# Another order for the gated update's candidate, root and gate steps, and a row of ones set inside the second loop

## The chip, the cores and the metric

One core of a Trainium2 chip runs the whole kernel in one launch. The metric is the time of the launch in device microseconds (us); the number that counts is the median of a few runs. Below, PE is TensorE, DVE is VectorE, ACT is ScalarE, POOL is GpSimd and SP is SyncE.

## The reference

Four graph layers on 3,125 nodes of 64 channels and 100,000 edges, with a layer norm of the residual behind each one: attention over edges (L0), an aggregation with a gated update (L1), a two-step convolution with small dense layers (L2), a relational layer (L3). The change sits at the end of L1, whose part that matters is:

```python
h = jnp.concatenate([xi, xj, ea], axis=-1) @ Wpre + bpre      # per edge
agg = jnp.concatenate([mean, mn, mx, std], axis=-1)           # over each node's edges
out = jnp.concatenate([m, o1, o2, o3], axis=-1) @ Wpost + bpost
gi = out @ Wih + bih
gh = x @ Whh + bhh
r = sigmoid(ir + hr); z = sigmoid(iz + hz)
n = tanh(i_n + r * h_n)                                       # the candidate
x = layernorm(x + (1.0 - z) * n + z * x)                      # its root: sqrt(var + eps)
```

## The kernel before

Nodes lie in 25 blocks of 128, one node per partition. An edge step handles up to 16 edges of each node of one block. The first loop runs over the steps for L0, the second one for L1; each turn does two steps (u = 0 and 1), 31 turns here. The second loop has two parts. Its first 25 turns also count edge types and unpack a matrix of counts, one block a turn, which ScalarE stores to DRAM (`at_tab`). The other 6 turns do not. In a step VectorE adds the gathered rows (L1983), signals GpSimd that the buffer is free, multiplies by the edge weight (L1987), adds TensorE's edge terms (L1995) and reduces the step before it (L1972, L1976). ScalarE makes maxima and minima (L1255). GpSimd gathers rows with indirect DMAs (L558), SyncE loads indices and attributes.

After the loop comes the chunk stage. The 25 blocks form three chunks of 8, 8 and 9 blocks. For each chunk:

- `sums_of` (DVE): mean, variance, minimum, maximum; ScalarE takes a root (`chunk_std`, L1274).
- `transpose_sums` and `mix_sums` (PE), with ScalarE's copies between them (`copy_sums`, L1096).
- `out_of` (DVE, L2049 to L2052): takes the products into `sR`.
- `transpose_out` (PE), `copy_out` (ACT, L1096) into the tile `T1`, then `gate_products` (PE, L696), two blocks to a product group. `T1` has 64 rows of data and a 65th row, `T1[C:C+1]`, that must be one for the bias.
- `take_gates` (ACT, L1294 and L1295): sigmoid and copy of each product group; this also frees the bank.
- `state_of` (DVE): the candidate's two steps (L2059, L2061), then `ask`, which signals ScalarE for the tanh (`chunk_tanh`, L1300) and waits for its answer; four steps of the update (L2063 to L2069); `layernorm` (L1893 to L1905), which asks ScalarE for the root (`std`, L1203) in its middle.
- `split` (DVE, L2075 to L2083): the new values in three bf16 parts for the convolution. Chunk 1's split lets TensorE begin the convolution (L916), chunk 2's lets it go on. At the end of the last `state_of` a signal (`x_done`) releases SyncE's next loads of `at_tab` (L523) and GpSimd's gathers of edge counts.

Each engine runs its instructions in the order in which they are written; an instruction that waits holds all behind it. ScalarE and VectorE meet by two counters (`act_q` up at each request, `act_r` at each answer), so requests must be answered in the order in which they are made. The order of the chunk stage is written out by hand on each engine. TensorE's order is: sums 0, mix 0, sums 1, mix 1, out 0, gates 0, sums 2, mix 2, out 1, gates 1, out 2, gates 2. ScalarE's function tables are reloaded when sigmoid or tanh follow the root, or the root them (ACT_TABLE_LOAD).

The memory of `T1` serves as workspace while counts are unpacked and stored, so its row of ones can be set only when the last store has landed (`at_stored`). Before the change VectorE sets it between `sums_of(2)` and `out_of(0)` (L2090, L2091), and then copies two small tables (`reset_loop`, L1803, L1804).

Of the kernel before, what the change touches and what calls it, by code (L numbers as in the profile page):

```python
# [32 lines left out]
N, E, C, R = 3125, 100000, 64, 9  # L33
NB = 25
# [25 lines left out]
def build(nc, a, out):  # L60
# [18 lines left out]
    with ExitStack() as ctx:  # L79
# [6 lines left out]
        def at(off, parts, *shape, dt=F32):  # L86
            n = 1
            for s in shape:
                n *= s
            v = arena[0:parts, off:off + n]  # L90
            if dt != F32:
                v = v.bitcast(dt)
            if len(shape) == 2:
                v = v.rearrange("p (a b) -> p a b", b=shape[1])
            if len(shape) == 3:
                v = v.rearrange("p (a b c) -> p a b c", b=shape[1], c=shape[2])
            return v
# [49 lines left out]
        gates = [at(14100 + 9 * 4 * C * c, P, 9, 4 * C) for c in range(3)]  # L147
# [14 lines left out]
        T1 = sb("T1", [P, NP])  # L162
# [147 lines left out]
        pack_in, pack_split, pack_cast, at_stored = (  # L310
            sem(n) for n in ("pack_in", "pack_split", "pack_cast", "at_stored"))
# [776 lines left out]
        def _(act):  # L1088
# [3 lines left out]
            def copy_transposed(dst, n, width):  # L1092

                k = ring["tp"]
                act.wait_ge(tp_full, k + 1)
                act.activation(dst, tp[0:width, k % 2, 0:n], ACT.Copy).then_inc(tp_evac, 1)  # L1096
                ring["tp"] = k + 1
# [5 lines left out]
            def asked():  # L1103
                act.wait_ge(act_q, ring["q"] + 1)
                ring["q"] += 1

            n = 0
# [40 lines left out]
            k = 1 + len(PAIRS)  # L1148
# [51 lines left out]
            def std(lo=0, hi=NB):  # L1200

                asked()
                act.activation(S(STD_)[:, lo:hi], S(VAR_)[:, lo:hi], ACT.Sqrt, bias=epsb[:], scale=1.0 / C).then_inc(  # L1203
                    act_r, 1)
# [71 lines left out]
            def copy_sums(c):  # L1276
                lo = CHUNKS[c][0][0]
                for h in range(2):
                    for g in CHUNKS[c]:
                        copy_transposed(aggT[h][:, (g[0] - lo) * P:(g[-1] + 1 - lo) * P], P * len(g), P)  # L1280
# [5 lines left out]
            def take_gates(c, first, last):  # L1286
                lo = CHUNKS[c][0][0]
                for k in range(first, last):
                    pair = CHUNK_PAIRS[c][k]
                    bank = MM_GRU[c] + k  # L1290
                    b = slice(pair[0] - lo, pair[-1] + 1 - lo)
                    v = mm[:, bank % 2].rearrange("p (b c) -> p b c", c=4 * C)[:, 0:len(pair)]
                    act.wait_ge(mm_full, bank + 1)
                    act.activation(gates[c][:, b, 0:2 * C], v[:, :, 0:2 * C], ACT.Sigmoid)  # L1294
                    act.activation(gates[c][:, b, 2 * C:], v[:, :, 2 * C:], ACT.Copy).then_inc(mm_evac, 1)  # L1295

            def chunk_tanh(c):
                s = slice(CHUNKS[c][0][0], CHUNKS[c][-1][-1] + 1)
                asked()
                act.activation(sR[:, s], sR[:, s], ACT.Tanh).then_inc(act_r, 1)  # L1300
# [6 lines left out]
            copy_out(0)  # L1307
            act.wait_ge(sums_done, AGG + 2)
            take_gates(0, 0, 4)
            copy_sums(2)  # L1310
            copy_out(1)
            take_gates(1, 0, 4)
            chunk_tanh(0)
            copy_out(2)
            take_gates(2, 0, 3)
            std(0, 8)
            take_gates(2, 3, 5)
            chunk_tanh(1)
            std(8, 16)
            chunk_tanh(2)  # L1320
            std(16, 25)

# [53 lines left out]
            for s in range(NB):  # L1376
# [3 lines left out]
                for gi, g in enumerate(GROUPS):  # L1380
                    n = len(g)
# [33 lines left out]
        def _(dve):  # L1415
# [11 lines left out]
            def ask(ins):  # L1427

                ins.then_inc(act_q, 1)
                ring["q"] += 1  # L1430
                dve.wait_ge(act_r, ring["q"])
# [120 lines left out]
            for pair in PAIRS:  # L1552
                s = ring["stage"] % NSTAGE
                if ring["stage"] >= NSTAGE:
                    dve.wait_ge(stage_out[s], 16 * (ring["stage"] // NSTAGE))
                n = len(pair)
                k = ring["mm"]
# [360 lines left out]
            for half, done in zip(HALVES, (X1A, X1)):  # L1918
                lo, hi = half[0][0], half[-1][-1] + 1
                w = slice(lo, hi)  # L1920
                for g in half:
                    n = len(g)
# [56 lines left out]
            def step1(i, u, with_hist):  # L1979
                blk = block_in(word[u])  # L1980
                h = hh[u][:, :, 0:C]
                wait_rows(LOOP1, u)
                tt(h, G1[u], aR[:, bass.ds(blk, 1), :].to_broadcast([P, SLOTS, C]), ALU.add).then_inc(index_used, 1)  # L1983
                dve.wait_ge(attrs_in[u], 16 * (i + 1))
                prepare_step(2 * i + u + 1, 1 - u)
                d().then_inc(LOOP1.free, 1)
                tt(h, h, bc(ewm[u], C), ALU.mult)  # L1987
                tt(rel_hot[:], bc(relation[u], R), bm(relF[:], SLOTS), ALU.is_equal)
                d()
                red_(rel_sum[:], rel_hot[:].rearrange("p s r -> p r s"), X_AXIS, ALU.add)  # L1990
                d()
                v_ = accT[:, bass.ds(blk, 1), :]
                tt(v_, v_, rel_sum[:].unsqueeze(1), ALU.add)
                dve.wait_ge(edge_terms, 2 * i + u + 1)
                tt(h, h, mm[:].rearrange("p a (s c) -> p (a s) c", c=C), ALU.add).then_inc(h_ready, 1)  # L1995
                if with_hist:
                    type_hots(1, 2 * i + u + 2 * HI, 8 * (2 * i + u) + 16 * HI, u)
                if with_hist and u == 0:
                    dve.wait_ge(pack_in, 16 * (i + 1))
                    dve.wait_ge(pack_cast, i + 1)  # L2000
                    ts(even_sb, pack_sb, 0x070707, None, op0=ALU.bitwise_and)
                    ts(odd_sb, pack_sb, 3, 0x071F1F, op0=ALU.logical_shift_right, op1=ALU.bitwise_and)
                    ts(top_sb, pack_sb[:, 0:P], 22, 3, op0=ALU.logical_shift_right, op1=ALU.bitwise_and)
                    d().then_inc(pack_split, 1)
                add_step(2 * i + u, 1 - u)
                end_step(u)

            with aligned(dve, 0, HI) as i:
                for u in range(2):
                    step1(i, u, True)  # L2010
            with dve.Fori(HI, pairs) as i:
                for u in range(2):
                    step1(i, u, False)
# [8 lines left out]
            def range_of(c):  # L2022
                lo, hi = CHUNKS[c][0][0], CHUNKS[c][-1][-1] + 1
                return slice(lo, hi), hi - lo
# [17 lines left out]
            def out_of(c):  # L2042
                s, n = range_of(c)
                for k, g in enumerate(CHUNKS[c]):
                    bank = MM_AGG[c] + k
                    dve.wait_ge(mm_full, bank + 1)
                    w = slice(g[0], g[-1] + 1)
                    v = mm[:, bank % 2].rearrange("p (b c) -> p b c", c=2 * C)[:, 0:len(g)]
                    tt(mpR[:, w], mpR[:, w], v[:, :, 0:C], ALU.add)  # L2049
                    tt(sR[:, w], v[:, :, C:2 * C], bc(S(RATIO_)[:, w], C), ALU.mult).then_inc(mm_evac, 1)  # L2050
                d()
                tt(sR[:, s], sR[:, s], mpR[:, s], ALU.add)  # L2052
                d().then_inc(sums_done, 1)

            def state_of(c):
                s, n = range_of(c)
                gate = lambda k: gates[c][:, 0:n, k * C:(k + 1) * C]
                dve.wait_ge(mm_evac, MM_GRU[c] + len(CHUNK_PAIRS[c]))
                tt(sR[:, s], gate(0), gate(3), ALU.mult)  # L2059
                d()  # L2060
                tt(sR[:, s], sR[:, s], gate(2), ALU.add)  # L2061
                ask(d())
                tt(gate(0), x1R[:, s], sR[:, s], ALU.subtract)  # L2063
                d()
                tt(gate(0), gate(0), gate(1), ALU.mult)
                d()
                tt(gate(0), gate(0), sR[:, s], ALU.add)
                d()
                tt(sR[:, s], gate(0), x1R[:, s], ALU.add)  # L2069
                d()  # L2070
                layernorm(xN, sR, s.start, s.stop, scrC)
# [15 lines left out]
            ts(totI[:, 2:3], l3[:, 2, 0:1], float(E), None, op0=ALU.is_lt)  # L2087
            for c in range(3):
                sums_of(c)
            dve.wait_ge(at_stored, 16 * (NB + 1))  # L2090
            dve.memset(T1[C:C + 1], 1.0)  # L2091
            reset_loop()
            for c in range(3):
                out_of(c)
            ring["mm"] = MM_MLP[0]
            for c in range(3):
                state_of(c)
                if c == 2:
                    d().then_inc(x_done, 1)
                s, n = range_of(c)  # L2100
                split(parts2[:, s], xN[:, s], scrC[:, 0:n])
# [169 lines left out]
```

## Time and profile before

| | |
|---|---|
| median of 3 runs | 3,403.16 us (3,392.29 to 3,418.53) |
| the profiled execution's own time | 3,406.42 us |
| its span, first to last instruction | 3,404.6 us |
| busy: DVE, POOL, PE, ACT | 2,097.6, 1,803.9, 1,468.5, 1,244.7 us |
| mean granted clock of TensorE | 0.615 of full speed |
| border of the second loop's two parts | near 2,697 us |
| chunk stage | about 2,934 to 3,049 us |

The profile shows one execution. Its times count from the first instruction. A busy share is an average over stages with different limits, so what an edit is worth has to be read in its own stage, from the chain of waits and the timeline.

### The profile page before, as it was taken

What the parts mean: (1) busy time and instruction counts of PE and PEld (TensorE: products, weight loads), DVE (VectorE), ACT (ScalarE), POOL (GpSimd) and SP (SyncE); (2) the same over time, 40 slices, a digit from 0 to 9 for tenths busy, and PEclk for the clock granted to TensorE, in tenths of its full rate; (3) what the DMA queues carried; (4) which work ended last, traced back from release to release, by engine and by line L of the source; (5) the groups of instructions that cost most, each with busy time, mean ns of one, the idle gap of its engine ahead of it and who ended that gap; (6) DMA issues with size and microseconds to landing.
All of it is one profiled execution on the core that took longest, in us unless ns stands there. A gap on an engine that the chain in (4) does not pass through costs nothing.

```text
span 3404.6 us, 29222 instructions
## 1 busy us (share of the span) xinstructions
PE 1468.5 (43%) x4582; PEld 640.3 (19%) x4583; DVE 2097.6 (62%) x3689; ACT 1244.7 (37%) x3273; POOL 1803.9 (53%) x1818
## 2 busy tenths in 40 slices
PE   3124444455433443334133344443332322467996
PEld 2001111111111111113011111111111100366553
DVE  5736666677645555567466678885665656642456
ACT  0013333333322333343255556663544445321122
POOL 3366666666666666660666666666666666011011
PEclk9986666566656555666555555555555555568986
DMA  5222221222212212220111122221111111016320
GB/s 126 68 50 50 51 49 46 51 51 48 55 46 55 48 46 52 53 56 14 37 50 49 49 52 61 53 51 49 47 49 49 37 24 24 32 59 204 128 71 6
DMA packets 124348, 186.68 MB, mean 55 GB/s; under 512 B 62045, under 2 KB 79154, under 8 KB 124127
## 3 DMA queue, kind: packets, MB, share of 16 engines
q0 software_dynamic: 57776, 89.59, 12.5%
q1 hardware_dynamic: 48894, 70.70, 6.6%
q10 hardware_dynamic: 17618, 25.71, 2.1%
q8 instruction: 23, 0.38, 0.0%
q14 instruction: 37, 0.30, 0.0%
HBM read 146.04 MB, written 39.84 MB: 55 GB/s over the span
## 4 chain that ended last, share of the span: by engine, by line
DVE 26%; issue 22%; PE 18%; DVEq 14%; ACT 9%; another core or an unknown queue 9%; ACTq 1%; POOL 1%; DMA 0%; POOLq 0%; SPq 0%
ACT arena L1255 6%; DVE arena L1854 4%; PE mm L696 4%; PE mm L838 4%; DVE red L1972 4%; DVE red L1868 3%; PE hist L916 2%; DVE score L1834 2%; DVEq L1750 2%; DVEq L1867 2%; PE hist L778 2%; PE l L987 2%; PE l L756 2%; DVE T L1825 1%
## 5 line engine op out<-in xcount | busy, mean ns | idle before, releaser
L558 POOL DMA_INDIRECT arena<-b_tab,lin x815 | 815.3, 1000 | 554.1 <-issue 351.8
L558 POOL DMA_INDIRECT arena<-kv_tab,rec x815 | 819.5, 1006 | 392.9 <-issue 358.3
L756 PE MATMUL l<-arena,identB 128*128 128x512 bf16 x996 | 404.3, 570 | 641.6 <-DVE arena L1854 391.3
L1255 ACT ACTIVATE arena<-arena,lin 128x64 f32<-128x64 f32 x1984 | 504.5, 334 | 206.9 <-issue 206.7
L838 PE MATMUL mm<-Wslots,eaT 48*128 48x512 f32 x248 | 234.2, 1097 | 673.5 <-ACT eaT L1249 326.1
L1972 DVE TENSOR_REDUCE red<-arena 128x128 f32<-128x2048 f32 x189 | 459.4, 2487 | 13.9 <-issue 13.0
L1854 DVE TENSOR_SCALAR arena<-arena,digit 128x512 bf16<-128x512 int16 x744 | 258.6, 418 | 188.1 <-remote 99.9
L756 PEld LDWEIGHTS l<-arena,identB 128*128 128x128 bf16 x996 | 114.9, 128 | 920.0 <-DVE arena L1854 458.4
L778 PE MATMUL hist<-arena,oh_lo 125*128 125x225 bf16 x400 | 170.7, 583 | 181.2 <-DVE arena L1825 151.9
L838 PEld LDWEIGHTS mm<-Wslots,eaT 48*128 48x128 f32 x248 | 72.2, 320 | 764.4 <-ACT eaT L1249 337.6
L1184 ACT ACTIVATE T<-arena,negcode 128x512 f32<-128x512 int16 x248 | 164.7, 711 | 139.5 <-remote 135.1
L1252 ACT ACTIVATE arena<-arena 128x1024 f32<-128x1024 f32 x62 | 65.5, 1057 | 398.1 <-DVE arena L1995 281.3
L1187 ACT ACTIVATE arena<-T,digit,negdigit 128x512 bf16<-128x512 f32 x248 | 188.4, 807 | 8.6
L561 POOL DMA_INDIRECT out<-arena,infoR x25 | 24.6, 985 | 292.2 <-DVEq L2182 239.7
L778 PE MATMUL hist<-T,oh_lo 125*128 125x225 bf16 x400 | 169.9, 581 | 11.2 <-issue 4.8
L1987 DVE TENSOR_TENSOR arena<-arena,lin 128x1024 f32<-128x1024 f32 x62 | 76.0, 1225 | 156.1 <-issue 150.9
L1178 ACT ACT_TABLE_LOAD x31 | 39.8, 1283 | 314.2 <-issue 170.1
L1983 DVE TENSOR_TENSOR arena<-arena 128x1024 f32<-128x1024 f32 x62 | 76.0, 1226 | 117.3 <-issue 98.3
L1834 DVE TENSOR_REDUCE score<-arena 128x64 f32<-128x1024 f32 x62 | 75.6, 1220 | 115.5 <-issue 113.1
L1995 DVE TENSOR_TENSOR arena<-arena,mm 128x1024 f32<-128x1024 f32 x62 | 75.7, 1221 | 113.4 <-PE mm L838 71.8
L1868 DVE TENSOR_REDUCE red<-arena 128x68 f32<-128x1088 f32 x62 | 130.1, 2098 | 9.2 <-issue 2.6
L778 PEld LDWEIGHTS hist<-arena,oh_lo 125*128 125x128 bf16 x400 | 53.8, 148 | 335.2 <-DVE arena L1825 214.7
(381 smaller groups left out, 2458.3 us busy)
## 6 DMA issues: line engine op xcount, KB each, us to landing
arena<-at_tab SPq DMA_DIRECT2D x50, 800.0 KB, 4.3
at_tab<-T ACTq DMA_DIRECT2D x25, 800.0 KB
arena<-kv_tab,rec POOLq DMA_INDIRECT x815
arena<-b_tab,lin POOLq DMA_INDIRECT x815
at_pack<-arena SPq DMA_DIRECT2D x25, 256.0 KB
T<-at_pack SPq DMA_DIRECT2D x25, 256.0 KB
lin_tab<-lin ACTq DMA_DIRECT2D x62, 64.0 KB
lin<-lin_tab SPq DMA_DIRECT2D x62, 56.0 KB
```

The lines of the kernel that those rows point to most:

```text
L558: return pool.indirect_dma_start(dst, None, table, offs(ap=index, axis=0))
L696: last = pe.matmul(mm[0:rows, k % 2, cols[0]:cols[1]], l, r, start=(t == 0), stop=(t == len(terms) - 1))
L756: last = pe.matmul(l3[:, 0, :], identB[:], hot[:, j], start=False, stop=True, skip_group_check=True)
L778: last = pe.matmul(hist[:, 0:NB * R], oh_lo[:, u, :, j], oh_hi[n][u][:, :, j], start=False, stop=True, skip_group_check=True)
L838: last = pe.matmul(mm[:, j, :], eaT[u], Wslots[:, 8 * j:8 * j + 8].rearrange("p s c -> p (s c)"), start=True, stop=True)
L1184: act.activation(distance[k], colI, ACT.Abs, bias=negcode[u][:, j + k:j + k + 1])
L1187: last = act.activation(onehotA[:, j + k], distance[k], ACT.Relu, scale=negdigit[u][:, j + k:j + k + 1], bias=digit[u][:, SLOTS - 4 + j + ...
L1255: last = act.activation(dst[:, s], hh[u][:, s, 0:C], ACT.Identity, bias=bias[:, s:s + 1])
L1834: red_(score[u][:], prod[:, :, 0:C].rearrange("p s (h c) -> p s h c", h=HEADS), X_AXIS, ALU.add)
L1854: last = ts(onehot[:, (u + q) % 2, j], colI, G[u][:, s, 2 * C:2 * C + 1], digit[u][:, s:s + 1], op0=ALU.is_equal, op1=ALU.mult)
L1868: red_(red[:, 0:C + HEADS], weighted[u].rearrange("p s c -> p c s"), X_AXIS, ALU.add)
L1972: red_(r, t.rearrange("p s c -> p c s"), X_AXIS, op)
```

## The change

ScalarE takes chunk 0's tanh right behind chunk 0's gates, and places the roots of the layer norm (`std`) between the gate groups of the next chunk, after its second group. VectorE's `state_of` is cut in two: `candidate_of` (both candidate steps and the request for the tanh) and the rest. Chunk 0's candidate now stands between `out_of(1)` and `out_of(2)`, the two table copies behind `out_of(2)`. The wait for the last store and the fill of the row of ones move from behind the chunk sums to between the second loop's two parts. TensorE, GpSimd and SyncE keep their instructions and order.

```diff
@@ ScalarE
             take_gates(0, 0, 4)
+            chunk_tanh(0)
             copy_sums(2)
             copy_out(1)
-            take_gates(1, 0, 4)
-            chunk_tanh(0)
+            take_gates(1, 0, 2)
+            std(0, 8)
+            take_gates(1, 2, 4)
             copy_out(2)
-            take_gates(2, 0, 3)
-            std(0, 8)
-            take_gates(2, 3, 5)
             chunk_tanh(1)
+            take_gates(2, 0, 2)
             std(8, 16)
+            take_gates(2, 2, 5)
             chunk_tanh(2)
             std(16, 25)
@@ VectorE, the second loop
             with aligned(dve, 0, HI) as i:
                 for u in range(2):
                     step1(i, u, True)
+            dve.wait_ge(at_stored, 16 * (NB + 1))
+            dve.memset(T1[C:C + 1], 1.0)
             with dve.Fori(HI, pairs) as i:
                 for u in range(2):
                     step1(i, u, False)
@@ VectorE, the chunk stage
-            def state_of(c):
+            def candidate_of(c):
                 s, n = range_of(c)
                 gate = lambda k: gates[c][:, 0:n, k * C:(k + 1) * C]
                 dve.wait_ge(mm_evac, MM_GRU[c] + len(CHUNK_PAIRS[c]))
...
                 tt(sR[:, s], sR[:, s], gate(2), ALU.add)
                 ask(d())
+
+            def state_of(c):
+                s, n = range_of(c)
+                gate = lambda k: gates[c][:, 0:n, k * C:(k + 1) * C]
                 tt(gate(0), x1R[:, s], sR[:, s], ALU.subtract)
...
             for c in range(3):
                 sums_of(c)
-            dve.wait_ge(at_stored, 16 * (NB + 1))
-            dve.memset(T1[C:C + 1], 1.0)
+            out_of(0)
+            out_of(1)
+            candidate_of(0)
+            out_of(2)
             reset_loop()
-            for c in range(3):
-                out_of(c)
             ring["mm"] = MM_MLP[0]
             for c in range(3):
+                if c:
+                    candidate_of(c)
                 state_of(c)
                 if c == 2:
                     d().then_inc(x_done, 1)
```

## Rows read from the trace of the kernel before

**Rows 1.** The chain of waits, chunk stage: start, us, what (x instructions).
```profile
2953.78 0.77 issue
2954.55 2.73 DVE T L2091
2957.29 0.18 DVE small L1803
...
2982.26 6.05 PE mm L696 x36
...
3003.74 10.51 PE mm L696 x48
...
3020.71 0.69 DVE arena L2059
...
3033.71 0.76 DVE arena L2059
...
3048.67 4.51 PE l L916 x27
...
3058.38 26.47 another core or an unknown queue
```

**Rows 2.** Timeline, chunk stage: start, us, engine, line [idle before, releaser].
```profile
2977.36 0.38 ACT L1295 ACTIVATE arena<-mm 128x256 f32<-128x256 f32 x1
2977.94 0.60 ACT L1096 ACTIVATE arena<-tp 128x512 f32<-128x512 f32 x1 [0.20 <-PE tp L680]
...
2989.90 0.69 DVE L2059 TENSOR_TENSOR arena<-arena 128x512 f32<-128x512 f32 x1
...
3001.77 0.63 ACT L1300 ACTIVATE arena<-arena 128x512 f32<-128x512 f32 x1
...
3002.44 0.69 DVE L2063 TENSOR_TENSOR arena<-x1R,arena 128x512 f32<-128x512 f32 x1 [11.07 <-ACT arena L1300]
...
3014.95 1.28 ACT L1203 ACT_TABLE_LOAD   x1
...
3016.58 0.20 DVE L1903 RECIPROCAL small<-small 128x8 f32<-128x8 f32 x1 [7.82 <-ACT small L1203]
...
3019.57 0.27 ACT L1295 ACTIVATE arena<-mm 128x128 f32<-128x128 f32 x1
```

**Rows 3.** Waits of VectorE, 2,957 to 3,034: total us, times, longest.
```profile
DVE arena L2049 <- PE mm L696: 25.2, 4, 20.2
```

**Rows 4.** Timeline behind the chunk stage.
```profile
3044.46 13.34 SPq L523 DMA_DIRECT2D arena<-at_tab  x6
...
3050.41 0.94 POOL L558 DMA_INDIRECT arena<-cnt_tab,infoR  x1 [153.66 <-issue]
```

**Rows 5.** Timeline of VectorE from the border of the second loop's parts.
```profile
2695.68 0.57 DVE L1976 TENSOR_TENSOR arena<-arena,red 128x128 f32 x3 [0.18 <-issue]
2697.18 1.23 DVE L1983 TENSOR_TENSOR arena<-arena 128x1024 f32<-128x1024 f32 x1 [0.94 <-issue]
2705.56 1.23 DVE L1987 TENSOR_TENSOR arena<-arena,lin 128x1024 f32<-128x1024 f32 x1 [7.15 <-issue]
...
2710.38 1.22 DVE L1995 TENSOR_TENSOR arena<-arena,mm 128x1024 f32<-128x1024 f32 x1 [2.54 <-PE mm L838]
...
2746.98 1.23 DVE L1987 TENSOR_TENSOR arena<-arena,lin 128x1024 f32<-128x1024 f32 x1 [11.23 <-issue]
```

**Rows 6.** Stretches: us, busy PE, PEld, DVE, ACT, POOL, clock, DMA share, GB/s.
```profile
2685.00:2687.00 2.00, 0.38 (x1) 0.00 (x0) 1.59 (x2) 0.33 (x1) 1.42 (x2) 0.50 0.16 28
...
2964.00:2969.00 5.00, 4.28 (x38) 4.01 (x37) 1.45 (x3) 2.12 (x3) 0.00 (x0) 0.99 0.00 0
...
2990.00:2993.00 3.00, 3.00 (x27) 3.00 (x28) 1.28 (x2) 0.66 (x2) 0.00 (x0) 0.97 0.00 0
...
3004.00:3019.00 15.00, 15.00 (x72) 15.00 (x72) 6.42 (x12) 5.50 (x11) 0.00 (x0) 0.50 0.01 2
```

**Rows 7.** DMA queues, 2,697 to 2,933: packets, MB, share of 16 engines.
```profile
q14 instruction: 2, 0.02, 0.0%
```

## The prediction, made before the changed kernel ran

> **What bounds the kernel now.** The views were read in this order: the page, for the whole; the chain of waits from 2,950 to 3,060 us, for which engine ends each step there; the timeline of the same stretch, for who waits for whom; the waits of VectorE, for their sums; the table of stretches, for TensorE's clock; and the timeline around the border of the loop's two parts.
>
> The whole span is long (3,404.6 us) and the edited chunk stage is a small part of it, about 2,934 to 3,049 us. No engine bounds the whole. In the chunk stage the chain runs over VectorE's sums, the row of ones (2.73 us, with 0.77 us of nothing before it), then TensorE's products for one chunk after another, and from 3,016 us on over VectorE alone, until the last part of chunk 2 releases the convolution at 3,048.67 [rows 1]. The reader is to see that TensorE's last gate product ends near 3,019 and ScalarE has emptied it at 3,019.84 [rows 2], while VectorE starts on chunk 2's candidate only at 3,033.71 [rows 1]. VectorE has a queue of work at the end, and idled before: 20.2 us for chunk 2's products [rows 3], 11.07 us for chunk 0's tanh, 7.82 us for chunk 0's root [rows 2]. The tanh waited for nothing but its place in ScalarE's order: its input was there at 2,991.4 (the first candidate step starts at 2,989.90 and two of 0.7 us follow each other), and it ran at 3,001.77, behind chunk 1's gates [rows 2]. The root's input was there at 3,008.8 (6.3 us after the 3,002.44 of the row) and it ran near 3,016.25, behind three pairs of chunk 2's gates and a table load [rows 2].
>
> **The change, step by step.**
>
> Row of ones leaves the chunk stage. VectorE's first output step began at 2,957.47 (2,957.29 and 0.18). Without the fill and with the two reset copies behind chunk 2's output, it can begin at 2,953.85, when the chunk sums are signalled [rows 1]: 3.6 us earlier. If the 0.77 us ahead of the fill stays, it is 2.9. I take 3.6, since nothing in the trace claims that gap but the fill. TensorE's second mix and chunk 0's gates move with it, for it waited for these steps to empty its bank.
>
> Chunk 0's tanh now stands between chunk 0's gates and chunk 2's transposed sums on ScalarE, so these copies wait for VectorE's candidate. VectorE is idle there (the 20.2 us), so the price is the candidate's own length: two steps of 0.69 us, the hand-over and the tanh of 0.63, some 2.1 us from the last gate copy (2,977.36 and 0.38) [rows 2]. Behind it ScalarE's six copies used to take 4.3 us (2,977.94 to 2,982.2), with waits for transposes in them; two banks are full by then, so they need some 3.9. The second chunk's mix, at 2,982.26 before, is therefore 1.7 us late in its own frame (0 to 2.2). Net shift of TensorE from there: 3.6 - 1.7 = 1.9 us earlier.
>
> From there, in the times of the old trace less 1.9: chunk 2's output steps end at 2,987.9 (2,989.90 before [rows 2], at which the next step started); the two reset copies, now here, take 0.3. VectorE goes straight on with chunk 0, whose tanh is long there: variance 6.4 us later, at 2,994.7. ScalarE has taken two pairs of chunk 1's gates by 2,993.2 and reloads the root's table (1.28 us [rows 2]) while it waits; root at 2,995.0. The rest of chunk 0 with its split took 4.1 us (3,016.58 to 3,020.71 [rows 1, 2]): free at 2,999.2. Chunk 1's gates are out at 3,000.0, its candidate and tanh end near 3,002.3 (behind the copies of chunk 2's output), its variance at 3,008.6. There ScalarE first takes the second pair of chunk 2's gates (ready about 3,008.8) and loads the table, so the root comes at 3,011.1, a new wait of some 2.4 us on VectorE, and split 1 ends at 3,015.1. Both waits lie ahead of what now ends last: chunk 2's candidate needs all of chunk 2's gates, which ScalarE has out at 3,019.84 less 1.9, less 0.1 for the tanh no longer ahead of the output copies: 3,017.85. From there to the release of the convolution it is the old chain of 14.96 us (3,033.71 to 3,048.67 [rows 1]). Result: 3,017.9 instead of 3,033.7, **15.8 us earlier**. With no shift at all it would be 13.8; so the bulk does not hang on the first two steps. What is late next is TensorE's gate products: VectorE now waits 2.7 us for them.
>
> The table loads: there were a load for the root, one back for sigmoid, one for the root, one for tanh, one for the root; now root, sigmoid, root, sigmoid, root. Five either way, each 1.28 us; the load row begins 0.01 us behind the last gate copy, with nothing between [rows 2]. The Trainium skill (ScalarE: Activation LUTs, What ACT_TABLE_LOAD costs) states 2.66 us for a switch, with a drain of 1.38 us beside the load. By that the root of chunk 1 would come 1.4 us later, split 1 would end at 3,016.5, and the sum would stay 15.8, as 3,017.9 still ends last; the row shows no such drain.
>
> Behind the stage. The last part of state 2 releases the queue that loads the convolution's tiles (3,044.46) and, 6.0 us later, GpSimd's 25 gathers (first at 3,050.41) [rows 4]; the convolution then starves for 26.47 us behind them [rows 1]. Both hang on the same event as the release, so the stretch moves as a block: cost 0, between 0 and a few us if its collisions fall otherwise. The tile loads that can start earlier were started by the chunk sums and are done.
>
> The row of ones in the loop. VectorE now stands still between the two parts for the wait and 2.73 us. Its last step there ends at 2,696.25 (2,695.68 and 0.57 [rows 5]). The wait is for the last store of counts, whose traffic has fallen to 28 GB/s by 2,685 to 2,687 [rows 6], 9 us before; it costs nothing. What queues behind the fill: the addition at 2,697.18, which hands the buffer back to GpSimd's gathers and the index slot to SyncE, and then the product that began only at 2,705.56 after 7.15 us of slow issue [rows 5]. The sum that follows waits 2.54 us for TensorE (2,710.38 [rows 5]), which itself waited for ScalarE. So 2.8 us falls into 7.15 or into 2.54 us of slack. I take 0.3 us; ends 0 and 2.9, the latter if the slow issue lengthens by all of it.
>
> Sum: -15.8 + 0.3 = **-15.5 us**. The profiled execution took 3,406.42 us and would take 3,390.9. The median of the runs shown (3,403.16) is 3.3 us below it, which gives **3,388 us**.
>
> **Rivals.**
>
> A, the clock gives part back. Chunk 0's gates ran at 0.99 for 5 us and chunk 2's at 0.50 throughout [rows 6], that is 2.4 and 1.2 GHz. If the fast stretches (4.3 us of products near 2,964, 3.0 near 2,990) fall to the low level, TensorE ends some 7 us later, and it is TensorE that bounds now: gain 8.5, 3,395 us. For it: TensorE is now nearly without pause here. Against: that order of its work is the same.
>
> B, the clock helps. If chunk 2's gates run at the high level (15.6 us become 8), VectorE bounds: its own work of 13.0 and 14.96 us behind 2,999.2 ends at 3,027; gain 21, 3,382 us. For it: fewer pauses of TensorE before. Against: rows 6.
>
> C, the gain is given back behind the stage. If the convolution's loads collide worse with the gathers, the 26.47 us [rows 1] grow by the 15: 3,403 us. Against: both start from one event, at a fixed distance.
>
> D, slower. The added instructions push the second part of the loop along in VectorE's code, so that its jump back finds its code not there. The mechanism's price from the nearest row: GpSimd, whose next code lay behind a skipped branch, took 6.0 us from the event to its first gather [rows 4]. Five jumps back of the second part would cost 30 us: 3,418 us; it decides from three such stalls on. Against: in all turns of the second part the instruction queue moved only 2 packets [rows 7], so the jumps back find their code now, and slow issue of up to 11.23 us [rows 5] was there without any fetch. The Trainium skill (Runtime: NRT & Kernel Launch, Instruction fetch mechanics) says that a taken branch whose target lies outside the pages held forces a fetch before it goes on; the trace agrees in that no jump here does so yet, and by the rule the second part turns dear only if the few added instructions move a turn over one page border more.
>
> **How the numbers follow.** Chances: forecast 0.60, A 0.17, B 0.10, C 0.08, D 0.05. The runs shown lie between 3,392.29 and 3,418.53, 0.8% apart, so even a median of three moves by several us; the forecast's own ends (gain 10 to 17 with the bounds above) are 3,386 to 3,393. Range: B's 3,382 less 7 for the scatter, 3,375, up to 3,402 just short of C. A change of 1% is 34 us, about what can be told from none here. No case reaches it; only scatter or an effect unseen in these rows does: faster 0.05, within 1% 0.92, slower 0.03.
>
> **What would show it.** In the new trace: no fill near 2,954 and VectorE's output steps 3 to 4 us earlier against the end of the chunk sums; chunk 0's tanh directly behind chunk 0's gates; from the first mix's end to the release of the convolution 15 to 16 us less; VectorE's 11.07 and 7.82 us gone, and a wait of 2 to 3 us each before chunk 1's root and before chunk 2's candidate, the latter for ScalarE's last gate copy. At the border of the loop's parts a fill of 2.7 us with the next sum waiting less than 2.5 us for TensorE. The prediction is wrong if chunk 2's candidate starts more than 1 us after its last gate copy (VectorE still bounds), if that copy comes later than 66 us after the end of the chunk sums, or if the 26.47 us stretch grows.

## The result, and the profile after

| | before | after |
|---|---|---|
| median of 20 runs each | 3,403.3 us (3,390.5 to 3,420.8) | 3,394.7 us (3,364.3 to 3,406.9) |
| ratio, 95% interval | | 0.996 (0.9942 to 0.9977): 13.6 us less (7.8 to 19.7) |
| the same pair again, on another occasion | 3,443.8 us | 3,425.5 us; 0.9946 (0.9925 to 0.9967): 18.6 us less |
| profiled execution: span | 3,404.6 us | 3,384.3 us |
| chunk stage, signal of the sums to release of the convolution | 94.9 us | 79.1 us |

In the last row the signal is the end of ScalarE's last root over the chunk sums, on which VectorE waits, and the release is the first product of the convolution behind chunk 2's split.

The kernel became faster by 0.4%, within 1%. The forecast was 15.5 us; both comparisons hold it in their intervals. The forecast of the median, 3,388 us, is 6.7 us below the 3,394.7 measured. The two medians of the first comparison differ by only 8.6 us; its runs scatter by up to 1.3%, so the ratio is the better reading. The two profiled spans differ by 20.3 us, of which the chunk stage gives 15.8; of the rest 5.4 us lie ahead of the signal, less than the runs of one kernel differ (30 us before), and behind the release 0.9 us were lost.

First the chain of waits of the kernel after, from the last chunk sum to the convolution (start, us, what), which answers to [rows 1]:

```profile
2948.30 0.03 issue
2948.34 0.08 issue
2948.43 0.42 DVE arena L2052
...
2970.41 0.63 ACT arena L1300
...
2974.89 7.16 PE mm L696 x36
...
2983.64 10.18 PE mm L696 x64
...
2996.37 15.63 PE mm L696 x72
...
3012.50 0.76 DVE arena L2062
...
3027.46 4.50 PE l L916 x27
...
3037.49 25.70 another core or an unknown queue
```

The reader is to see that the row of ones and the 0.77 us ahead of it are both gone: 0.1 us from the signal to the first output step instead of 3.7. The chain now runs through chunk 0's tanh and then through TensorE up to chunk 2's candidate; VectorE's own work ends it only over the last 15 us. From 2,948.34 to 3,027.46 are 79.1 us; before, from 2,953.76 (in [rows 1] the gap that follows starts at 2,953.78) to 3,048.67, 94.9.

The timeline of VectorE and ScalarE (idle time and its releaser in brackets), which answers to [rows 2]:

```profile
2968.88 0.69 DVE L2062 TENSOR_TENSOR arena<-arena 128x512 f32<-128x512 f32 x1 [11.91 <-ACT arena L1295]
...
2970.41 0.63 ACT L1300 ACTIVATE arena<-arena 128x512 f32<-128x512 f32 x1 [1.56 <-DVEq L2065]
...
2978.78 0.42 DVE L2052 TENSOR_TENSOR arena<-arena,mm 128x256 f32<-128x256 f32 x1 [8.43 <-PE mm L696]
...
2990.89 0.20 DVE L1904 RECIPROCAL small<-small 128x8 f32<-128x8 f32 x1 [0.40 <-ACT small L1203]
...
3005.80 0.21 DVE L1904 RECIPROCAL small<-small 128x8 f32<-128x8 f32 x1 [2.30 <-ACT small L1203]
...
3012.20 0.27 ACT L1295 ACTIVATE arena<-mm 128x128 f32<-128x128 f32 x1
3012.50 0.76 DVE L2062 TENSOR_TENSOR arena<-arena 128x576 f32<-128x576 f32 x1 [2.70 <-ACT arena L1295]
```

Chunk 0's tanh stands behind its gates and is done 0.7 us behind VectorE's request, within the 8.43 us in which VectorE waits for chunk 2's products anyway, so nothing is left of the 11.07 us. The root's 7.82 us became 0.4. A wait of 2.3 us before chunk 1's root and one of 2.7 us before chunk 2's candidate are new. The candidate starts 0.03 us behind the last gate copy.

The timeline of VectorE at the border of the loop's parts, which answers to [rows 5]:

```profile
2694.19 0.56 DVE L1977 TENSOR_TENSOR arena<-arena,red 128x128 f32 x3 [0.18 <-issue]
2695.70 2.73 DVE L2013 MEMSET T<- 1x3200 f32 x1 [0.95 <-issue]
2699.57 1.23 DVE L1984 TENSOR_TENSOR arena<-arena 128x1024 f32<-128x1024 f32 x1 [1.14 <-issue]
2706.95 1.23 DVE L1988 TENSOR_TENSOR arena<-arena,lin 128x1024 f32<-128x1024 f32 x1 [6.16 <-issue]
...
2710.47 1.22 DVE L1996 TENSOR_TENSOR arena<-arena,mm 128x1024 f32<-128x1024 f32 x1 [1.24 <-PE mm L838]
```

The sum with TensorE's terms comes 15.7 us behind the last addition of part one instead of 14.1.

### The profile page after: what moved, and what is told of

The parts are those of the page before. It is cut to its first block, busy times and chain, and to the rows that moved or that the text cites. A ratio compares the mean times of both kernels' runs of the same rounds, so it can differ in the third digit from the quotient of the medians.

```text
span 3384.3 us, 29223 instructions
## 1 busy us (share of the span) xinstructions
PE 1464.7 (43%) x4582; PEld 639.0 (19%) x4583; DVE 2095.3 (62%) x3689; ACT 1243.6 (37%) x3273; POOL 1811.3 (54%) x1818
## 4 chain that ended last, share of the span: by engine, by line
DVE 25%; issue 23%; PE 18%; DVEq 14%; ACT 10%; another core or an unknown queue 7%; ACTq 1%; POOL 1%; DMA 0%; POOLq 0%; SPq 0%
ACT arena L1255 6%; DVE arena L1855 4%; PE mm L696 4%; PE mm L838 4%; DVE red L1869 4%; DVE red L1973 3%; PE hist L916 2%; DVEq L1868 2%; DVE score L1835 2%; DVEq L1751 2%; PE l L756 2%; PE l L987 2%; PE hist L778 2%; DVE T L1826 1%
## 5 line engine op out<-in xcount | busy, mean ns | idle before, releaser
L558 POOL DMA_INDIRECT arena<-kv_tab,rec x815 | 828.3, 1016 | 326.1 <-issue 290.9
L1973 DVE TENSOR_REDUCE red<-arena 128x128 f32<-128x2048 f32 x189 | 459.3, 2485 | 13.7 <-issue 12.7
L1184 ACT ACTIVATE T<-arena,negcode 128x512 f32<-128x512 int16 x248 | 164.5, 710 | 19.7 <-remote 11.1
L558 POOL DMA_INDIRECT rec<-rec_tab,win x63 | 61.8, 981 | 143.8 <-issue 122.8
```

Of the source, the lines that this page charges most:

```text
L558: return pool.indirect_dma_start(dst, None, table, offs(ap=index, axis=0))
L1184: act.activation(distance[k], colI, ACT.Abs, bias=negcode[u][:, j + k:j + k + 1])
L1973: red_(r, t.rearrange("p s c -> p c s"), X_AXIS, op)
```

## The experiments

Their kernels are compared with the kernel before on the same chip and occasion. Most ran where the kernel before takes 2,955 us, the second pair above and two more where it takes 3,444 us (the last section says what differs). So absolute times are not compared across them; the stage, read between two marks within one trace, is. In these ten kernels the whole run moved by what the stage moved, within the interval (in us, whole run from the ratio; four fills and one gather are told with their experiments):

| kernel | stage | less than 94.9 | whole run less (95%) |
|---|---|---|---|
| row alone | 91.6 | 3.3 | 2.1 (-0.6 to 4.7) |
| order alone | 82.5 | 12.4 | 12.1 (8.0 to 16.0) |
| the change again | 79.2 | 15.7 | 18.6 (11.4 to 25.8) |
| tanh behind copies | 77.7 | 17.2 | 15.7 (11.5 to 19.5) |
| roots late | 93.0 | 1.9 | 2.7 (0.0 to 5.3) |
| two products | 75.1 | 19.8 | 20.1 (16.3 to 24.2) |
| tanh behind copies, two products | 66.2 | 28.7 | 28.1 (23.6 to 32.5) |
| tanh behind copies, work in waits | 71.4 | 23.5 | 25.5 (16.9 to 34.4) |
| tanh behind copies, three products | 69.5 | 25.4 | 21.4 (12.7 to 30.0) |
| tanh behind copies, three products, work in waits | 66.6 | 28.3 | 26.6 (22.5 to 30.4) |

**The row of ones alone.** The fill and its wait moved as in the change, all else as before.

```diff
+            dve.wait_ge(at_stored, 16 * (NB + 1))
+            dve.memset(T1[C:C + 1], 1.0)
             with dve.Fori(HI, pairs) as i:
...
-            dve.wait_ge(at_stored, 16 * (NB + 1))
-            dve.memset(T1[C:C + 1], 1.0)
```

> The kernel before with the row of ones alone moved to between the loop's two parts; ScalarE's and VectorE's order in the chunk stage as before. The stage is read from the end of the last chunk root (sums signalled) to the release of the convolution by chunk 2's split: 94.9 us before, 79.1 us after the whole change. Forecast's theory: the first output step starts 0.1 us behind the signal instead of 3.7 us, all that follows moves by 3.6 us, the stage takes 91.3 us and the whole run is 3.3 us shorter. Rival 1, the 0.77 us ahead of the fill belongs to something else: 92.1 us. Rival 2, the stage's end does not hang on the outputs: 94.9 us.

The stage took 91.6 us; the first output step began 0.32 us behind the signal, since the two table copies are still there. The 0.77 us belonged to the fill.

**The order alone.** The changed kernel, its fill put back behind the sums.

```diff
             for c in range(3):
                 sums_of(c)
+            dve.wait_ge(at_stored, 16 * (NB + 1))
+            dve.memset(T1[C:C + 1], 1.0)
             out_of(0)
```

> The changed kernel with the row of ones back behind the chunk sums; the new order kept. Forecast's theory: the order alone is worth 12.2 us, the stage takes 82.7 us (79.1 and the 3.6 of the fill), the second chunk's mix starts 1.7 us later against the signal of the sums than before the change, and chunk 2's candidate starts within 0.5 us of its last gate copy. Rival, order and row are not additive, because what ends last changes with them: the stage is near 79 us (the fill costs nothing when TensorE's gates bound otherwise) or above 86 us.

82.5 us, and its 12.4 with the row's 3.3 make 15.7: the two add. Chunk 2's candidate starts 0.03 us behind its last gate copy. The mix that was to be 1.7 us late starts 29.84 us behind the signal instead of 28.50: 1.3 late.

**Chunk 0's tanh behind the copies.**

```diff
-            chunk_tanh(0)
             copy_sums(2)
+            chunk_tanh(0)
```

> The changed kernel with chunk 0's tanh behind the copies of chunk 2's transposed sums instead of ahead of them. Forecast's theory: the tanh ahead of the copies holds TensorE back by 1.7 us and TensorE's gates set the stage's end, so the third mix starts 1.7 us earlier and the stage takes 77.4 us. Rival, VectorE's own chain sets the end already, or the copies need no less time: 79.1 us.

77.7 us; the third mix starts at 25.1 instead of 26.6 us behind the signal. The price of the tanh's place was real, 1.5 us, and it reached the end of the stage, so TensorE sets that end.

**The roots in their old places.**

```diff
-            take_gates(1, 0, 2)
-            std(0, 8)
-            take_gates(1, 2, 4)
+            take_gates(1, 0, 4)
             copy_out(2)
-            chunk_tanh(1)
-            take_gates(2, 0, 2)
-            std(8, 16)
-            take_gates(2, 2, 5)
-            chunk_tanh(2)
+            take_gates(2, 0, 3)
+            std(0, 8)
+            take_gates(2, 3, 5)
+            chunk_tanh(1)
+            std(8, 16)
+            chunk_tanh(2)
```

> The changed kernel with the roots of the layer norm in ScalarE's old places (chunk 0's behind three pairs of chunk 2's gates, chunk 1's behind its tanh), the tanh of chunk 0 early as in the change. Theory: the early tanh without an early root only moves VectorE's wait; the root of chunk 0 comes at about 61 us behind the signal of the sums, then VectorE's own 32 us follow, and the stage takes 93 us, 1.8 us below the kernel before. Rival, the early tanh is what gives the time (it had the longer wait, 11.07 against 7.82 us): the stage takes 79 to 85 us.

93.0 us. The timeline of this kernel at chunk 0's root (as above):

```profile
2587.05 0.30 ACT L1203 ACTIVATE small<-small,epsb 128x8 f32<-128x8 f32 x1
...
2587.39 0.20 DVE L1903 RECIPROCAL small<-small 128x8 f32<-128x8 f32 x1 [20.09 <-ACT small L1203]
```

VectorE runs ahead and waits 20.1 us for the root in place of 11.07 and 7.82. The 1.9 us below the kernel before are not the tanh's: this kernel has the row of ones moved too, and with the row alone the stage took 91.6 us. So the early tanh alone loses 1.4 us, its price for TensorE, and gives nothing back. Of the two waits in one chain, both had to go.

**The fill four times over**, with a drain between two, at the same place of the changed kernel.

```diff
             dve.memset(T1[C:C + 1], 1.0)
+            d()
+            dve.memset(T1[C:C + 1], 1.0)
... (three times)
```

> The changed kernel with the row of ones filled four times over at the border of the loop's parts (4 x 2.73 us, with a drain between two). Read from the end of the last addition of part one to the start of the first sum with TensorE's edge terms in part two: 14.1 us before, 15.7 us after the change. Theory: the spell of slow issue there lasts until a time of its own, so the fills eat its 6.2 us and then the 1.2 us of waiting for TensorE: 8.2 us more cost 1 us, and the stretch takes 16 to 17 us. Rival, the slow issue is counted in instructions and comes behind the fills undiminished: 22 to 23 us.

Neither theory: there was no spell of slow issue in this execution (the only one: 2,944.2 us, the kernel before 2,955.6). The sum with TensorE's terms came 17.7 us behind the last addition, 10.5 us later than with one fill (7.3) and 10.7 later than with none (7.0). VectorE's timelines at the border, first of the kernel with the order alone (no fill there):

```profile
2314.14 0.57 DVE L1977 TENSOR_TENSOR arena<-arena,red 128x128 f32 x3 [0.18 <-issue]
2318.16 1.23 DVE L1984 TENSOR_TENSOR arena<-arena 128x1024 f32<-128x1024 f32 x1 [3.45 <-DMA arena<-b_tab,lin]
...
2335.75 1.23 DVE L1984 TENSOR_TENSOR arena<-arena 128x1024 f32<-128x1024 f32 x1 [4.86 <-DMA arena<-b_tab,lin]
...
2512.58 0.39 DVE L2021 COPY histo<-hist 128x225 f32<-128x225 f32 x1
```

then of the kernel with four fills:

```profile
2328.36 2.73 DVE L2019 MEMSET T<- 1x3200 f32 x1 [0.76 <-issue]
2331.10 1.23 DVE L1984 TENSOR_TENSOR arena<-arena 128x1024 f32<-128x1024 f32 x1
...
2344.80 1.27 DVE L1984 TENSOR_TENSOR arena<-arena 128x1024 f32<-128x1024 f32 x1 [0.69 <-issue]
...
2515.80 0.39 DVE L2029 COPY histo<-hist 128x225 f32<-128x225 f32 x1
```

VectorE waits 3.45 us at the border for gathered rows, and 4.86 us more a step later. One fill fits into the first wait: the next addition comes 3.7 us behind the border with it and 3.45 without. Four fills take the next step's wait too, and by the end of part two, 12 steps on, 1.0 us of their 10.7 is left (from 2,314.71 to 2,512.58 are 197.9 us, from 2,316.95 to 2,515.80 198.9; with one fill 197.9 again). What hides the fill is GpSimd's gathers, which set the pace of the second part: with no fill VectorE waits 34.3 us for their rows there, with four 18.3.

**One gather instead of 25.** The counts of the other blocks are left as they lie, so the relational layer computes with other numbers. VectorE's wait for the counts is lowered to match (not shown).

```diff
-            for b in range(NB):
-                gather(cntR[:, b, 0], cnt_tab, infoR[:, b, 0:1]).then_inc(cnt_in, 16)
+            gather(cntR[:, 0, 0], cnt_tab, infoR[:, 0, 0:1]).then_inc(cnt_in, 16)
```

> The changed kernel with one of the 25 gathers of edge counts behind the chunk stage; the other blocks' counts are left as they lie in memory, so part of the relational layer is computed with other numbers. Theory: the convolution starves for 25.7 us because the loads of its tiles share the DMA engines with the 25 gathers; without them the stretch from the release of the convolution to its fifth block's sum shrinks from 35.7 us to below 15 us and the run is 15 to 25 us shorter. Rival, the loads are slow for another reason (their release, their own queue): the stretch keeps more than 30 us.

Inconclusive. The fifth block's sum came 8.9 us behind the release, but in the run with the row alone, with all 25 gathers, it came after 9.3; the ratio, 0.9949 (0.9936 to 0.9963), is that of the changed kernel. There was no starved stretch to take away on this occasion. The run with the row alone shows that 25 gathers side by side with the loads do not by themselves starve the convolution.

**The change again.** The changed kernel, for the comparison on the chips of the experiments.

> The changed kernel itself, beside the kernel before on one chip of the kind on which the experiments ran, where the kernel before takes 2,955 us. The forecast's sum there: the stage 94.9 less 15.8 us, so near 79.1 us; at the border of the loop's parts 0.2 us later; the whole run 15.5 us shorter, 2,939 to 2,940 us, ratio 0.9948. Rival, part of the stage's gain is lost behind it as the median of the first comparison (8.6 us) suggests: 2,945 to 2,948 us.

It met an occasion on which the kernel before takes 3,444 us, so the 2,939 us can't be read; the stage took 79.2 us and the ratio is 0.9946. The rival, a loss behind the stage, finds no support: the whole run lost no less than the stage (18.6 us, 11.4 to 25.8), and from the release to the end it was 357.1 us, against 356.0 in the trace of the kernel before.

**Two gate products per block.** The weights are padded with zeros to 256 columns, the order of the four parts is changed with them, and VectorE reads the parts in their new places (neither shown).

```diff
-                        parts += [(P, (o, o + 2 * C), [(xb, Whh[:, 0:2 * C]), (ob, Wih[:, 0:2 * C])]),
-                                  (P, (o + 2 * C, o + 3 * C), [(ob, Wih[:, 2 * C:])]),
-                                  (P, (o + 3 * C, o + 4 * C), [(xb, Whh[:, 2 * C:])])]
+                        parts += [(P, (o, o + 4 * C), [(xb, Whh[:]), (ob, Wih[:])])]
```

> The changed kernel with two gate products per block instead of four (the weights padded with zeros to 256 columns, so that one product makes all from x and one all from the output; same result). It halves TensorE's instructions in the gates. Forecast's theory, TensorE's gates set the stage's end: chunk 0's gates end some 5.8 us earlier, the later two shrink by 5 and 7.8 us, and then VectorE's own chain bounds; the stage takes 69 us instead of 79.1, and chunk 2's candidate no longer waits for gates. Rival, VectorE or ScalarE bounds already: the stage stays above 77 us. Rival 2, the clock falls or the wider products take as long as two: 74 to 79 us.

Rival 2: 75.1 us. Chunk 2's gates took 15.7 us, no less than the 15.6 with four products. In the timeline of TensorE of this kernel a product (two records) starts 0.85 us after the one before at the low clock:

```profile
2575.71 1.06 PE L696 MATMUL mm<-Whh,T 65*128 65x256 f32 x2
2576.57 1.06 PE L696 MATMUL mm<-Wih,T 65*128 65x256 f32 x2
```

A block costs 2 x 0.85 = 1.7 us, as much as four narrower products of 0.43. Of the 4.1 us gained 3.4 came in chunk 0's gates (7.8 us instead of 11.2) and the rest before the third mix, and both are bound up with the clock: it was at 1.00 through these gates and the transposes behind them, where with four products it was at 0.66 and 0.50.

**Both edits together**: two products per block, and the tanh behind the copies.

> Two gate products per block and chunk 0's tanh behind the copies, together. If both theories hold: the third mix 1.7 us earlier than with two products alone, VectorE's own chain behind it, the stage takes 67 to 68 us and the whole run is 11 to 12 us shorter than the changed kernel. Rival, chunk 0's tanh is late for VectorE now that TensorE is fast, and it eats the gain: 69 us or more.

66.2 us, 13.0 less than the change's 79.2, where the two edits gave 4.1 and 1.5 alone. The clock was high through chunk 1's gates (1.00 over the 10 us from 2,558, which is 2.4 GHz). Stretches: us, busy PE, PEld, DVE, ACT, POOL, granted clock, DMA share, GB/s; first with two products alone, then with both edits.

```profile
2560.00:2572.00 12.00, 12.00 (x37) 9.53 (x37) 9.15 (x16) 5.50 (x11) 0.00 (x0) 0.60 0.00 1
```

```profile
2558.00:2568.00 10.00, 7.74 (x40) 6.43 (x38) 8.23 (x15) 6.27 (x14) 0.00 (x0) 1.00 0.00 1
```

**Work in TensorE's waits.** Products of zeros where TensorE waits for ScalarE's copies (17 by the edit; the expectation says 15), the tanh behind the copies.

```diff
+            def keep_busy(n):
+                for _ in range(n):
+                    pe.matmul(l3[:, 0, :], zerosb[:, 0:P], zerosb[:], start=True, stop=True)
...
                     for k, g in enumerate(CHUNKS[c]):
+                        if c == 2 and (h, k) == (0, 2):
+                            keep_busy(4)
...
+                if c == 2:
+                    keep_busy(2)
...
                 for k, g in enumerate(CHUNKS[c]):
+                    if k == 2:
+                        keep_busy(2)
                     transpose_group([sR[:, b] for b in g])
+                keep_busy(3)
```

> Chunk 0's tanh behind the copies, as in the third experiment, and TensorE given 15 products of zeros (128x512, into a bank that is free) in the places where it waits for ScalarE's copies; the result is not touched. In the third experiment its clock was at 0.5 from 22.9 to 40.0 and from 46.8 us on behind the signal of the sums, and the stage took 77.7 us; with both edits together it was at 1.0 from 15.7 to 49.8 and the stage took 66.2. Theory: TensorE's short waits are what lets the clock fall, so with work in them it stays high through chunk 1's gates, VectorE's own chain bounds, and the stage takes 66 to 70 us. Rival, the clock falls whatever stands in the waits, and the added products cost 2 to 4 us: 79 to 82 us.

71.4 us, between the two, and 6.3 below the same kernel without these products, which compute nothing. The cause is the clock: chunk 1's gates took 8.6 us instead of 11.0, chunk 2's 12.3 instead of 15.6, with the same products at a higher mean clock. Stretches (as above) of chunk 1's and chunk 2's gates, first without the products of zeros, then with them:

```profile
2565.40:2576.40 11.00, 10.94 (x65) 10.94 (x66) 9.11 (x18) 4.85 (x10) 0.00 (x0) 0.65 0.00 1
2579.00:2594.50 15.50, 15.48 (x73) 15.49 (x74) 9.26 (x16) 5.98 (x12) 0.00 (x0) 0.50 0.00 1
```

```profile
3009.40:3018.00 8.60, 8.60 (x65) 8.60 (x66) 7.06 (x14) 4.28 (x8) 0.00 (x0) 0.84 0.00 1
3021.90:3034.20 12.30, 12.30 (x75) 12.29 (x74) 9.57 (x17) 6.13 (x12) 0.00 (x0) 0.64 0.00 0
```

That the waits alone let it fall is not shown; it still was low for part of each.

**Three gate products per block** of 192, 128 and 64 columns, the tanh behind the copies.

```diff
+                        parts += [(P, (o, o + 3 * C), [(xb, Whh[:, 0:3 * C])]),
+                                  (P, (o, o + 2 * C), [(ob, Wih[:, 0:2 * C])], True),
+                                  (P, (o + 3 * C, o + 4 * C), [(ob, Wih[:, 3 * C:])])]
```

The `True` marks a product that adds to what lies in the bank. The padding and the order of the parts change as for two products (not shown).

> Chunk 0's tanh behind the copies, and three gate products per block (192, 128 and 64 columns) instead of four (128, 128, 64, 64); same result. With two products of 256 columns the gates of chunk 2 took 15.8 us at the low clock, no less than with four: each record took 0.44 us against 0.21. Theory, a product costs by its columns but not below what 128 columns cost: a block takes 2 x (0.32 + 0.21 + 0.21) = 1.5 us at the low clock instead of 1.7, chunk 2's gates 13.4 instead of 15.6 us, and the stage takes 72 to 74 us if the clock stays as in the third experiment, 66 if it stays high. Rival, the time goes by the number of products alone: gates of 11.7 us, a stage of 68 to 70 at the low clock; or by columns alone: 384 columns either way, no change, 77.7.

69.5 us. Chunk 2's gates took 13.7 us, near the theory's 13.4, and there the clock was at 0.50 throughout, as in the kernel with the tanh behind the copies alone (15.6 us). So 1.9 us of the 8.2 gained over that kernel are the products'. The other 6.3 came earlier, where the clock was higher too (chunk 1's gates 6.4 us at 1.00 instead of 11.0 at 0.65), and how they divide stays open.

**All that helped.** Three products, work in the waits, the tanh behind the copies.

> All that helped so far: chunk 0's tanh behind the copies, three gate products per block, and products of zeros in TensorE's waits. Alone the last two gave stages of 69.5 and 71.4 us. VectorE's own chain is the floor: root 1 came at 46.1 us behind the signal in the run with both edits of the seventh experiment, and 4.1 us of split and 15.0 us of chunk 2 behind it make 65.2 us. Theory, the gains add until that floor: 65.2 to 66.5 us, chunk 2's candidate no longer waits for gates, and the run is 13 to 14 us shorter than the changed kernel. Rival, chunk 2's gates run at the low clock all the same and still set the end: 68 to 70 us.

66.6 us, ratio 0.991 to the kernel before: with the kernel of two products and the late tanh the fastest here (2,927.6 and 2,927.9 us, where the kernel before takes 2,956). The floor was missed by 1.4 us. Of that 1.0 arose early: the third mix starts 21.2 us behind the signal, in the kernel of the seventh experiment 20.2, and VectorE's chain behind it is later by as much (chunk 0's root at 34.3 instead of 33.3 us). There the transposes ahead of the mix ran at a clock of 1.00, here the first of them at 0.50. Another 0.3 us is the root's own time, which the floor left out. The chain of waits of this kernel, from chunk 1's variance on:

```profile
2577.90 0.69 DVE small L1918
2578.65 0.30 ACT small L1217
2578.97 1.28 ACT L1308
2580.26 0.38 ACT arena L1308
2580.65 0.28 ACT arena L1309
2580.98 1.77 PE mm L696 x6
2582.77 0.28 ACT arena L1308
2583.04 0.18 ACT arena L1309
2583.24 0.76 DVE arena L2078
```

ScalarE waits in the root's place for VectorE, and the gate copy behind it waits with it; TensorE, out of banks, waits 4.8 us for that copy before its last products. With TensorE fast, the early root holds it back. Here that costs the stage only 0.1 us, since VectorE is busy with chunk 1's split until 0.25 us ahead of chunk 2's candidate (the usual step between them is 0.1).

## Why the prediction was right

- **The fill leaves the stage, 3.6 us.** Right to 0.1 us: 3.74 to 0.14 us behind the signal in the profiles, 3.3 us of stage for the row alone and 3.3 between the two kernels that differ by it. The choice between 2.9 and 3.6, on the ground that nothing else claimed the gap, was the right one.
- **The tanh holds TensorE back by 1.7 us, net shift 1.9.** The third mix starts 26.55 us behind the signal after and 28.5 before: 1.95. The experiments put the price at 1.3 (order alone) and 1.5 (tanh behind the copies).
- **The waits move and shrink.** The forecast times, counted from the signal at 2,953.85, and what the profile after shows: chunk 0's root done at 41.2, measured 42.5; chunk 1's at 57.3, measured 57.4; wait for it 2.4, measured 2.3; last gate copy 64.0, measured 64.1; wait for it 2.7, measured 2.7. One step was mis-sized and another made up for it: the third mix took 7.16 us instead of 6.05 and chunk 1's gates 10.18 instead of 11.28, since the high clock fell on the gates in place of the mix (mean clock of the mix 0.58 instead of 0.69, of the gates 0.70 instead of 0.63). That the two cancel within 0.1 us was luck; the forecast held the clock fixed.
- **Nothing is lost behind the stage.** It was put at 0. From the release to the end it was 356.0 us before and 356.9 after, and the starved stretch 26.5 and 25.7 us. But the sentence that the convolution starves *behind* the gathers was argued from their lying side by side. The same gathers ran on other occasions with no starved stretch, so the cause is open.
- **The fill in the loop, 0.3 us.** The size holds (nothing left of one fill, 1.0 us left of 10.7 with four), the reason does not. The cover was sought in slow issue and TensorE's lateness; both are absent where the kernel runs in 2,955 us, and the fill is hidden there all the same, by the wait for gathered rows. Where slow issue was there, the next sum came 1.6 us later than before, and part two ended 235.6 us behind the border against 237.5. The same loop took 237.6 to 238.8 us in the three later traces of that kind, so a cost of a few tenths can be neither seen nor excluded there.
- **The rivals.** The medians alone would have spoken for A (8.6 us less; A says 8.5, 3,395 us). The trace excludes it: the stage lost 15.8 us, and chunk 2's gates took the same 15.62 us at 0.50 as before. A and B were both about the clock, and the clock did not move enough for either in the change itself; the experiments show that it was the live question: products of zeros alone took 6.3 us off. C and D did not occur: the instruction queue's packets rose by one in the whole run (37 to 38).

## What to carry over

When an engine waits for another one that has work queued ahead of the answer, move the answer forward, but follow the chain to the next request: here the early tanh alone made the stage 1.4 us longer, and the tanh and the roots together gave 12 us. Read such an edit between two marks inside the stage, not from the span: the stage took 79.0 to 79.2 us in four traces of this order, while the whole run scatters by 1%. And before hiding work in a loop, ask what paces the loop: a wait for the pacing engine at the next step, not the idle time at the very place, is what takes it up.

## What was not expected of the hardware

The same kernel ran at three levels: 3,403 us in the first comparison, 2,955 us and, on a chip that had shown 2,956 before, 3,444 us later. The engines' busy times differ by some 2% at most; what differs is idle time at issue. ScalarE's maxima and minima (out<-in, count | busy us, mean ns | idle before, releaser), first in the kernel after on the first occasion, then in the kernel with the row alone at 2,955 us:

```profile
L1255 ACT ACTIVATE arena<-arena,lin 128x64 f32<-128x64 f32 x1984 | 504.5, 335 | 207.5 <-issue 207.1
```

```profile
L1255 ACT ACTIVATE arena<-arena,lin 128x64 f32<-128x64 f32 x1984 | 479.5, 333 | 0.0
```

At 3,403 us some 180 of the 1,984 start 1.4 us after the one before, instead of 0.24, in spells that VectorE's small instructions share. At 2,955 us there is none. The starved stretch of the convolution goes with it: the fifth block's sum came 35.7 to 37.3 us behind the release in all five traces above 3,380 us, and 8.0 to 9.3 us in all nine below 2,950. No edit brought it about, and nothing here shows its cause. Since it leaves the chunk stage alone (79.2 us at 3,426 us, 79.1 in the kernel with four fills at 2,944), the change is worth the same at each level.

TensorE's products in this stage cost by their columns from 128 on: 0.43 us at 128 and at 64 columns, 0.85 at 256, at the low clock. So four products of 128 and 64 columns and two of 256 take the same time.
